# The last network of a decoder: six layers as one stream of 192 groups instead of sections per layer

## The chip, the cores and the metric

One core of a Trainium2 chip runs the whole program. The metric is the device time of one execution in microseconds (us). Three executions of the kernel before took 3035.06, 3035.88 and 3041.49 us; their median is 3035.88 us.

## The reference, cut to what matters

The program is a decoder of twelve blocks over `x` of 4 batches x 256 tokens x 128 channels. Only the last block, `L3_ffn`, is changed. It repeats six layers, each with its own weights; all arithmetic is float32:

```
for i in range(6):
    x = attn_layer(shift_tokens(x), ...) + x      # 16 heads of 64, windows of 32 tokens
    x = ffn_layer(shift_tokens(x), ...) + x       # layernorm, W1 (128 x 682), a * gelu(gate), W2 (341 x 128)

attn_layer:
    q, k, v = split(x @ Wqkv[i])                  # 128 -> 3 x 1024
    q, k = l2norm(q) * qs, l2norm(k) * ks         # per head of 64
    q = q * cos * scale + rotate_half(q) * sin * scale      # k with 1 / scale
    k = k * cos * inv   + rotate_half(k) * sin * inv
    out = softmax(q @ k.T * 8, masked to the own and the former window) @ v
    return out @ Wo[i]                            # 1024 -> 128
```

`shift_tokens` takes the upper half of the channels from the token before. The batches don't touch each other anywhere in this block.

## The kernel before, in words

`l3_ffn` holds the six layers. Each is a sequence of sections (`nc.Block`), and between two sections all engines meet at a barrier. An engine runs its own instructions in order and waits on semaphores that the others raise.

1. **Shift** (lines 1844 to 1868): eight transposes of `xin` on TensorE, ScalarE and VectorE copy the halves of the channels into `xnT`.
2. **`attend`** (line 1940), one section with two parts. The first makes the projections in 16 steps (two halves of 512 columns x 8 tiles of 128 tokens). A step is a q, a k and a v matmul of 512 columns (lines 2094, 2099), two squares on ScalarE (2203), and on VectorE the sum of squares per head (2249), its guard, the reciprocal of its root (ScalarE's Sqrt is line 2208) and two multiplies that put the normed q and k into `unit` (2264). The second part walks 32 groups; a group is one pair of heads of one batch, and the loop runs over the pairs outside and the batches inside. A group is, on TensorE, four transposes of q and k as they are (2165), four transposes of `sin_rows` (2177), the mask and 8 score matmuls (2111, 2116), four transposes of the probabilities (2132) and 6 value matmuls (2148). GpSimd makes `sin_rows`, the halves swapped times the sine table (2075), and multiplies the probabilities by `inverse` (2082). VectorE takes the negated maximum (2271), multiplies by the cosine table (2275), adds the two turned parts (2282), copies the turned probabilities (124) and inverts the sums (2294). ScalarE does four Exp with their sums (2222) and stores the heads (122). Behind the last group come the out projections of the four batches, 16 matmuls each (2190), added to `xin` (2298). All the weights of the output and the GLU arrive during this section.
3. **Late shift and norm**: three matmuls with a shift matrix (1895 to 1897), then `norm` with its statistics on VectorE, a Sqrt on ScalarE and transposes (325), with 20 matmuls that keep TensorE busy (229).
4. **GLU**: `chunk_block` with six gate matmuls, Gelu on ScalarE (1916), six value matmuls, multiplies on VectorE (1919), and 24 down matmuls (1928).

The next `w_qkv` is loaded in section 3. PSUM has eight banks; in `attend` the projections use six for q and k and two for v, and the groups use three for turning, two for scores, two for the turned probabilities and one for the heads.

## Time and profile before

| | |
|---|---|
| median of three executions | 3035.88 us |
| the profiled execution, its own time | 3039.18 us |
| its span, first to last instruction | 3037.4 us |
| TensorE busy over the span | 2697.1 us (89%) |
| VectorE | 1861.4 us (61%) |
| ScalarE | 1445.9 us (48%) |
| GpSimd | 994.7 us (33%) |
| mean granted clock of TensorE | 0.938 |

The profile shows one execution. "PE" is TensorE's matmuls, "PEld" its weight loads, which run beside the matmuls, "DVE" VectorE, "ACT" ScalarE and "POOL" GpSimd. A float32 matmul stands as two instructions (two weight loads and two matmuls), a transpose as one. The duration of one instruction holds a fill and a drain that overlap with its neighbours, so what an instruction costs its engine when work is queued is the distance from its start to the next start. The bracket at the end of a row is idle time of the engine before it and what ended it. The clock is the share of full speed (2.4 GHz) that TensorE was granted.

### The profile page before, as it was taken

The page shows a single profiled execution, that of the slowest core. Times are in us where ns is not written, and L with a number is a line of the kernel's source. Part 1 is how long each engine was busy: PE and PEld are TensorE (multiplying, and loading weights), DVE is VectorE, ACT ScalarE, POOL GpSimd, SP SyncE. Part 2 cuts the span into 40 slices and gives each one's busy share as a digit, 9 for nine tenths or more (in the row PEclk, how much of TensorE's full clock was granted, in tenths as well). Part 3 has the DMA queues.
Part 4 walks back from the last instruction along what each step waited for, and adds up shares of the span by engine and source line. Part 5 has one row for each costly group of instructions (what it writes and reads, how often), then busy time and mean ns, then how long its engine had stood idle before and what let it go on. Part 6 is the DMA issues. An engine that isn't in the chain of part 4 may idle for free. (4 is left out here: it accounts for less than half of the span.)

```text
span 3037.4 us, 59204 instructions
## 1 busy us (share of the span) xinstructions
PE 2697.1 (89%) x20645; PEld 1729.4 (57%) x20645; DVE 1861.4 (61%) x4106; ACT 1445.9 (48%) x4868; POOL 994.7 (33%) x1103
## 2 busy tenths in 40 slices
PE   5999969799989889783899978999999999999898
PEld 3555546455556556462455544856847647567476
DVE  3566665455567545556355558858677588586774
ACT  1455537326567456331255545545454355354553
POOL 0344435104456333100044431604406226044061
PEclk8799989898989999895799999999999999999999
DMA  2000000000000000000000001010010010100100
GB/s 66 1 0 0 0 8 2 20 26 1 5 1 2 4 28 0 6 1 7 26 1 0 0 32 46 2 46 19 12 53 2 22 42 2 49 15 23 42 2 29
DMA packets 41958, 48.85 MB, mean 16 GB/s; under 512 B 11963, under 2 KB 31301, under 8 KB 40838
## 3 DMA queue, kind: packets, MB, share of 16 engines
q1 hardware_dynamic: 41734, 45.89, 5.3%
q8 instruction: 138, 2.26, 0.3%
q14 instruction: 86, 0.70, 0.1%
HBM read 32.76 MB, written 0.52 MB: 11 GB/s over the span
## 5 line engine op out<-in xcount | busy, mean ns | idle before, releaser
L2075 POOL TENSOR_TENSOR net_sin_rows<-net_unit_qk,net_sin_table 128x512 f32<-128x512 f32 x192 | 243.8, 1270 | 649.8 <-PE bank L2177 375.3
L2222 ACT ACTIVATE net_probs<-bank,net_negmax 128x96 f32<-128x96 f32 x768 | 251.0, 339 | 302.4 <-DVE net_negmax L2271 302.4
L1022 POOL TENSOR_TENSOR l_probs<-l_probs,rowinv 128x512 f32<-128x512 f32 (+2 forms) x256 | 192.4, 772 | 571.8 <-DVE rowinv L1034 571.0
L1042 DVE TENSOR_REDUCE negmax<-scores 128x1 f32<-128x508 f32 (+4 forms) x512 | 212.8, 467 | 220.0 <-PE scores L919 180.2
L1022 POOL TENSOR_TENSOR lora_probs<-lora_probs,rowinv 128x508 f32<-128x508 f32 (+1 forms) x256 | 149.5, 617 | 253.3 <-DVE rowinv L1034 253.3
L987 ACT ACTIVATE l_probs<-scores,negmax 128x512 f32<-128x512 f32 (+2 forms) x256 | 139.5, 550 | 169.8 <-DVE negmax L1042 169.0
L124 DVE COPY turned<-flip 128x512 f32<-128x512 f32 (+3 forms) x280 | 163.0, 582 | 75.5 <-PE flip L946 65.9
L2094 PE MATMUL bank<-net_w_qkv,xnT 128*128 128x512 f32 x384 | 196.8, 637 | 7.5 <-PEq L1845 7.2
L734 DVE TENSOR_REDUCE negmax<-scores 128x2 f32<-128x256 f32 (+2 forms) x192 | 157.8, 822 | 66.3 <-PE scores L642 36.7
L919 PE MATMUL scores<-kT,qM 64*128 64x512 f32 (+2 forms) x768 | 190.2, 572 | 6.3 <-ACT kT L122 2.3
L987 ACT ACTIVATE lora_probs<-scores,negmax 128x508 f32<-128x508 f32 (+1 forms) x256 | 117.8, 472 | 132.2 <-DVE negmax L1042 131.4
L2082 POOL TENSOR_TENSOR net_probs<-net_probs,net_inverse 128x384 f32<-128x384 f32 x192 | 158.8, 827 | 51.6 <-DVE net_inverse L2294 51.6
L122 ACT ACTIVATE turned<-flip 128x512 f32<-128x512 f32 (+3 forms) x280 | 143.3, 512 | 59.2 <-PE flip L656 49.1
L2271 DVE TENSOR_REDUCE net_negmax<-bank 128x4 f32<-128x384 f32 x192 | 106.6, 555 | 104.2 <-PE bank L2116 104.2
L969 PE MATMUL heads<-turned,V 128*64 128x256 f32 (+1 forms) x1280 | 166.3, 381 | 2.0 <-ACT turned L122 1.3
L2116 PE MATMUL bank<-net_qk_T 64*64 64x96 f32 (+1 forms) x3072 | 162.5, 246 | 0.0
L2222 ACT ACTIVATION_READ_ACCUMULATOR net_probs<-bank,net_negmax 128x1 f32 x768 | 156.1, 203 | 0.0
L2116 PEld LDWEIGHTS bank<-net_qk_T 64*64 64x64 f32 x3072 | 125.7, 135 | 51.1 <-issue 51.1
L2177 PE MATMUL bank<-ident,net_sin_rows 128*128 128x128 f32 x768 | 121.5, 283 | 35.5 <-DVE net_cos_T L2275 35.3
L2203 ACT ACTIVATE net_probs_turned<-bank 128x512 f32<-128x512 f32 x192 | 114.0, 597 | 80.4 <-PE bank L2094 80.4
L124 DVE COPY net_probs_turned<-bank 128x512 f32<-128x512 f32 x192 | 130.6, 680 | 27.2 <-PE bank L2132 27.2
L2282 DVE TENSOR_TENSOR net_qk_T<-bank,net_cos_T 128x512 f32<-128x512 f32 x192 | 132.8, 692 | 18.0 <-issue 0.4
(399 smaller groups left out, 6144.0 us busy)
## 6 DMA issues: line engine op xcount, KB each, us to landing
net_w_qkv<-in_L_ffn_Wqkv SPq DMA_DIRECT2D x7, 1536.0 KB, 6.6
net_vals_between<-net_vals SPq DMA_DIRECT2D x48, 192.0 KB, 2.5
net_w_out<-in_L_ffn_Wo SPq DMA_DIRECT2D x6, 512.0 KB
net_vals_between<-net_vals SPq DMA_DIRECT2D x48, 64.0 KB, 1.9
moe_w<-in_L_ffn_w13T SPq DMA_DIRECT2D x8, 256.0 KB, 2.7
net_w<-in_L_ffn_W SPq DMA_DIRECT2D x6, 341.0 KB
moe_w<-in_L_ffn_w2T SPq DMA_DIRECT2D x8, 128.0 KB, 2.2
ctx_tok<-in_ctx SPq DMA_DIRECT2D x1, 768.0 KB, 6.5
```

The lines of the kernel that those rows point to most:

```text
L124: return nc.vector.tensor_copy(dst, src)
L734: nc.vector.tensor_reduce(negmax[:, c:c + 2], scores[:, 2 * half:2 * half + 2, 0:nk], AX.X, ALU.max, negate=True).then_inc(maxed.sem, 1)
L919: last = nc.tensor.matmul(scores[:, 2 * qt + h, 0:nk], qM[rows, 0, t * P:(t + 1) * P], kT[rows, k0:k0 + nk], start=True, stop=cross)
L969: last = nc.tensor.matmul(heads[rows, q0 * P:QT * P], V[:, v0 + j, rows], turned[:, 2 * p + h, c0:c0 + w], start=(j == 0), stop=(j == part ...
L987: last = nc.scalar.activation(pr[:, slot(g, qt, h), k0:k1], scores[:, 2 * qt + h, k0:k1], ACT.Exp, bias=negmax[:, u * tail + w:u * tail + ...
L1022: last = nc.gpsimd.tensor_tensor(own, own, rowinv[:, u * tail + w:u * tail + w + 1].to_broadcast([P, k1 - k0]), ALU.mult)
L1042: last = nc.vector.tensor_reduce(negmax[:, u * tail + w:u * tail + w + 1], scores[:, 2 * qt + h, k0:k1], AX.X, ALU.max, negate=True)
L2075: nc.gpsimd.tensor_tensor(halves(sin_rows[:, g % 2, :, :, :]), halves(tiles_of_group(g))[:, :, ::-1, :], sin_table[:, :, :, :, :].rearrang ...
L2082: nc.gpsimd.tensor_tensor(prob_blocks(g), prob_blocks(g), part, ALU.mult).then_inc(shared.sem, 1)
L2094: nc.tensor.matmul(qk_bank(u, s), own, w_qkv[:, s * INNER + c * BANK:s * INNER + (c + 1) * BANK], start=True, stop=True).then_inc(filled.s ...
L2116: last = nc.tensor.matmul(bank[rows_of(h), SCORE_BANKS[g % 2], first:(w + 1) * KEYS], qk_T[rows_of(h), g % 3, 0, w * QB:(w + 1) * QB], qk_ ...
L2222: last = nc.scalar.activation(prob_blocks(g)[:, w, :], score_blocks(g)[:, w, :], ACT.Exp, bias=maxima[:, g % 4, w:w + 1], accum_out=sums[: ...
```

## The change

The six layers become one section, `stream`, of ticks. Tick s does, for group s, the scores, the maximum and the Exp, and besides it fixed shares of the work of other groups, each engine in a written order. A job is one batch of one layer; there are 24 jobs of 8 groups each, 192 groups in all, and the ticks run from -10 to 203. In every two ticks stands one step of 128 tokens x 512 columns of a later job's projections (q in the even tick, k and v in the odd one), and once in eight ticks the shift, the out projection, the late shift, the norm and the three parts of the GLU of one job, at ticks `SHIFT`, `OUT`, `LATE`, `ZT`, `GATES`, `BOTH`, `UPS` and `DOWN` of the job.

- The rotation is made on the rows, ahead of the turn and ahead of the division by the norm: VectorE multiplies the projection by the cosine table and, with halves swapped, by the sine table (`part`), GpSimd adds the two (`add_parts`) and multiplies each group by the inverse norms. One set of four transposes turns the sum, and one copy moves it from PSUM, on ScalarE for even and on VectorE for odd groups. The sine rows, their transposes, the multiply and the add behind the turn are gone.
- The inverse roots of the head norms (32 values per partition, once in four ticks) and of the layer norm (2 values per partition, once in eight) are made on GpSimd in 14 instructions each, every one waiting for the one before it (`inverse_root`). ScalarE's Sqrt and VectorE's reciprocals of norms are gone.
- The v matmul, the shift, the out projection, the late shift, the norm's turn and the GLU's matmuls share one PSUM bank, `spare`. `take_spare` makes TensorE wait until the user before has read it.
- q and k have one bank each, the turn has one, the turned probabilities have one.
- Gelu is one instruction of 768 columns per job, in the same queue as the Exp of every tick. The gates are first moved to SBUF with their bias.
- The tables per layer are made by GpSimd in three instructions. The matmuls that keep TensorE busy are gone. `w_qkv` is loaded in two halves of columns per layer.

The core of the diff (the removed lines are `attend` and the sections, printed above):

```diff
+def inverse_root(pool, src, floor, out, temp, step, before):
+    half, y, t = temp[:, 0, :], temp[:, 1, :], temp[:, 2, :]
+    done = [before]
+    def then(ins, last=False):
+        done[0] += 1
+        ins.then_inc(step.sem, 1)
+        if not last:
+            pool.wait_ge(step.sem, step.at(0, done[0]))
+    then(nc.gpsimd.tensor_scalar(half, src, floor, -0.5, ALU.max, ALU.mult))
+    then(nc.gpsimd.tensor_scalar(y.bitcast(I32), half.bitcast(I32), -0.5, ROOT_MAGIC, ALU.mult, ALU.add))
+    for r in range(3):
+        then(nc.gpsimd.tensor_tensor(t, y, y, ALU.mult))
+        then(nc.gpsimd.tensor_tensor(t, t, half, ALU.mult))
+        then(nc.gpsimd.tensor_scalar(t, t, 1.5, None, ALU.add))
+        then(nc.gpsimd.tensor_tensor(y if r < 2 else out, t, y, ALU.mult), last=(r == 2))
...
+    JOBS, PER = DEPTH * B, PAIRS
+    G, S = JOBS * PER, JOBS * 4
+    SHIFT, PROJ = -10, -8
+    SCALE, TURN, FLIP, VALUES = 2, 1, 2, 3
+    OUT, LATE, ZT, GATES, BOTH, UPS, DOWN = 12, 13, 15, 16, 17, 18, 19
+    TICKS = range(SHIFT, PER * (JOBS - 1) + DOWN + 1)
...
+        qk_bank = (bank[:, 0, :], bank[:, 1, :])
+        turn_bank, flip_bank = bank[:, 3, :], bank[:, 6, :]
+        heads = bank[:, 7, 0:N]
+        spare = bank[:, 2, :]
...
+            held = []
+            def take_spare():
+                for sig, count in held:
+                    pe.wait_ge(sig.sem, sig.at(0, count))
+            for s in TICKS:
+                u = at_tick(s, PROJ, 2, S)
+                if u is not None:
+                    m, c, t = step_of(u)
+                    l, b = job(m)
+                    if u % 4 == 0:
+                        pe.wait_ge(shift_lower.sem, shift_lower.at(0, m + 1))
+                        pe.wait_ge(shift_upper.sem, shift_upper.at(0, m + 1))
+                    if b == 0 and t == 0:
+                        pe.wait_ge(qkv_in[c].sem, qkv_in[c].at(l, 1))
+                    until(pe, parted, 2 * u - 1)
+                    nc.tensor.matmul(qk_bank[0], xnT[:, (QT * b + t) * P:(QT * b + t + 1) * P], w_qkv[:, half_cols(c)],
+                                     start=True, stop=True).then_inc(q_filled.sem, 1)
+                u = at_tick(s, PROJ + 1, 2, S)
+                if u is not None:
+                    m, c, t = step_of(u)
+                    l, b = job(m)
+                    own = xnT[:, (QT * b + t) * P:(QT * b + t + 1) * P]
+                    until(pe, parted, 2 * u)
+                    nc.tensor.matmul(qk_bank[1], own, w_qkv[:, INNER + c * BANK:INNER + (c + 1) * BANK],
+                                     start=True, stop=True).then_inc(k_filled.sem, 1)
+                    take_spare()
+                    nc.tensor.matmul(spare, own, w_qkv[:, 2 * INNER + c * BANK:2 * INNER + (c + 1) * BANK],
+                                     start=True, stop=True).then_inc(v_filled.sem, 1)
+                    held = [(v_copied, u + 1)]
                 g = s
                 if 0 <= g < G:
+                    until_copied(pe, g)
+                    until(pe, exped, g - 1)
...
+                g = s + TURN
+                if 0 <= g < G:
+                    m, c = group(g)
+                    pe.wait_ge(scaled.sem, scaled.at(0, g + 1))
+                    until_copied(pe, g - 1)
+                    for k in range(2):
+                        for q in range(QT):
+                            last = nc.tensor.transpose(turn_bank[:, (k * QT + q) * P:(k * QT + q + 1) * P],
+                                                       rope[:, m % 3, q, k, cols_of(c)], ident[:, :])
+                    last.then_inc(turned.sem, 1)
...
+                n = at_tick(s, BOTH, PER, JOBS)
+                if n is not None:
+                    take_spare()
+                    k = GT[2]
+                    nc.tensor.matmul(spare[0:k, 0:N], w1[:, GLU + 2 * P:GLU + 2 * P + k], znT[:, :], start=True, stop=True)
+                    nc.tensor.matmul(spare[0:k, N:2 * N], w1[:, 2 * P:2 * P + k], znT[:, :], start=True, stop=True).then_inc(both_made.sem, 1)
+                    held = [(gated_up, 3 * n + 1)]
...
+            def square(u, s, filled):
+                act.wait_ge(filled.sem, filled.at(0, u + 1))
+                until(act, reduced, u - 1)
+                nc.scalar.activation(squares[:, u % 2, s, :], qk_bank[s], ACT.Square).then_inc(squared.sem, 1)
...
+                n = at_tick(s, GATES, PER, JOBS)
+                if n is not None:
+                    act.wait_ge(gates_made.sem, gates_made.at(0, n + 1))
+                    until(act, gated_up, 3 * n)
+                    for j in range(2):
+                        affine("act", gelu[:, j, :], spare[:, j * N:(j + 1) * N], 1.0, vec[:, 5 + j:6 + j]).then_inc(gates_moved.sem, 1)
+                n = at_tick(s, BOTH, PER, JOBS)
+                if n is not None:
+                    k = GT[2]
+                    act.wait_ge(both_made.sem, both_made.at(0, n + 1))
+                    affine("act", gelu[0:k, 2, :], spare[0:k, 0:N], 1.0, vec[0:k, 7:8]).then_inc(gates_moved.sem, 1)
+                    act.wait_ge(gates_moved.sem, gates_moved.at(0, 3 * n + 3))
+                    nc.scalar.activation(gelu[:, :, :], gelu[:, :, :], ACT.Gelu).then_inc(gelued.sem, 1)
...
+            def add_parts(u, s):
+                m, c, t = step_of(u)
+                own = rope[:, m % 3, t, s, half_cols(c)]
+                pool.wait_ge(parted.sem, parted.at(0, 2 * u + s + 1))
+                nc.gpsimd.tensor_tensor(own, own, sin_parts[:, (2 * u + s) % 4, :], ALU.add).then_inc(added.sem, 1)
...
+            for s in TICKS:
+                g = s - 1
+                if 0 <= g < G:
+                    pool.wait_ge(inverted.sem, inverted.at(0, g + 1))
+                    part = inverse[:, g % 4, :].rearrange("p (w o) -> p w o", o=1).to_broadcast([P, BLOCKS, KEYS])
+                    nc.gpsimd.tensor_tensor(prob_blocks(g), prob_blocks(g), part, ALU.mult).then_inc(shared.sem, 1)
+                g = s + SCALE
+                if 0 <= g < G:
+                    m, c = group(g)
+                    j = g // 4
+                    pool.wait_ge(added.sem, added.at(0, 4 * j + 4))
+                    pool.wait_ge(rooted.sem, rooted.at(0, ROOT_OPS * (j + 1)))
+                    own = rope[:, m % 3, :, :, cols_of(c)].rearrange("p t s (h d) -> p (t s) h d", d=DH)
+                    factor = head_inv[:, j % 2, :].rearrange("p (ts h o) -> p ts h o", ts=4, o=1)[:, :, 2 * (c % 4):2 * (c % 4) + 2, :]
+                    nc.gpsimd.tensor_tensor(own, own, factor.to_broadcast([P, 4, 2, DH]), ALU.mult).then_inc(scaled.sem, 1)
+                j = at_tick(s, PROJ + 5, 4, S // 2)
+                if j is not None:
+                    pool.wait_ge(reduced.sem, reduced.at(0, 2 * j + 2))
+                    inverse_root(pool, head_sums[:, j % 2, :], 1e-24, head_inv[:, j % 2, :], head_temp, rooted, ROOT_OPS * j)
+                n = at_tick(s, LATE + 1, PER, JOBS)
+                if n is not None:
+                    pool.wait_ge(spread_in.sem, spread_in.at(0, n + 1))
+                    inverse_root(pool, ln_sum[:, :], LN_EPS, ln_inv[:, :], ln_temp, ln_rooted, ROOT_OPS * n)
+                u = at_tick(s, PROJ + 1, 2, S)
+                if u is not None:
+                    add_parts(u, 0)
+                u = at_tick(s, PROJ + 2, 2, S)
+                if u is not None:
+                    add_parts(u, 1)
...
+            def part(u, s):
+                m, c, t = step_of(u)
+                l, b = job(m)
+                if u % (4 * B) == 0 and s == 0:
+                    dve.wait_ge(tabled.sem, tabled.at(0, 3 * (l + 1)))
+                dve.wait_ge(squared.sem, squared.at(0, 2 * u + s + 1))
+                raw = qk_bank[s].rearrange("p (h d) -> p h d", d=DH)
+                nc.vector.tensor_tensor(rope[:, m % 3, t, s, half_cols(c)].rearrange("p (h d) -> p h d", d=DH), raw,
+                                        cos_table[:, l % 2, t, s:s + 1, :].to_broadcast([P, HB, DH]), ALU.mult)
+                until(dve, added, 2 * u + s - 3)
+                swapped = qk_bank[s].rearrange("p (h f d) -> p h f d", f=2, d=DH // 2)[:, :, ::-1, :]
+                table = sin_table[:, l % 2, t, s:s + 1, :].rearrange("p o (f d) -> p o f d", f=2).to_broadcast([P, HB, 2, DH // 2])
+                nc.vector.tensor_tensor(sin_parts[:, (2 * u + s) % 4, :].rearrange("p (h f d) -> p h f d", f=2, d=DH // 2), swapped, table,
+                                        ALU.mult).then_inc(parted.sem, 1)
...
+                g = s + TURN
+                if 0 <= g < G and g % 2 == 1:
+                    dve.wait_ge(turned.sem, turned.at(0, g + 1))
+                    until(dve, scored, g - 1)
+                    copy("dve", qk_T[:, g % 2, :, :].rearrange("p s n -> p (s n)"), turn_bank).then_inc(copied["dve"].sem, 1)
+                u = at_tick(s, PROJ + 2, 2, S)
+                if u is not None:
+                    j = u // 2
+                    dve.wait_ge(squared.sem, squared.at(0, 2 * u + 2))
+                    until(dve, rooted, ROOT_OPS * (j - 2) + 1)
+                    nc.vector.tensor_reduce(head_sums[:, j % 2, u % 2 * 2 * HB:(u % 2 + 1) * 2 * HB],
+                                            squares[:, u % 2, :, :].rearrange("p s (h d) -> p (s h) d", d=DH), AX.X,
+                                            ALU.add).then_inc(reduced.sem, 1)
...
```

## Rows read from the trace of the kernel before

**Rows 1.** Windows, one layer; per engine busy us (x instructions), PE clock, DMA share, GB/s

```profile
...
2222.00:2423.00 201.00, 188.20 (x1650) 128.78 (x1650) 141.94 (x290) 96.05 (x368) 66.98 (x65) 0.97 0.08 25
...
```

**Rows 2.** Windows of the same layer: projections, the 32 groups, the rest

```profile
...
2228.00:2276.00 48.00, 47.47 (x108) 18.95 (x108) 42.17 (x80) 31.17 (x64) 3.00 (x3) 0.97 0.22 61
2276.00:2393.00 117.00, 110.61 (x1376) 89.86 (x1377) 85.33 (x169) 55.52 (x291) 63.02 (x62) 0.97 0.02 4
2393.00:2429.00 36.00, 30.35 (x169) 20.20 (x167) 14.21 (x42) 9.37 (x13) 0.95 (x1) 1.00 0.12 44
...
```

**Rows 3.** Timeline, one group, TensorE's weight loads: start us, us, instruction

```profile
...
2333.29 0.64 PEld L2116 LDWEIGHTS bank<-net_qk_T 64*64 64x64 f32 x16 [0.26 <-issue]
...
2334.05 0.42 PEld L2132 LDWEIGHTS bank<-ident,net_probs 128*128 128x128 f32 x4
...
2334.63 0.20 PEld L2148 LDWEIGHTS bank<-net_probs_turned,net_vals 128*64 128x64 f32 x4 [0.17 <-issue]
...
2335.23 0.42 PEld L2165 LDWEIGHTS bank<-ident,net_unit_qk 128*128 128x128 f32 x4
...
2335.62 0.47 PEld L2177 LDWEIGHTS bank<-ident,net_sin_rows 128*128 128x128 f32 x4
...
2336.06 0.10 PEld L2111 LDWEIGHTS bank<-net_window,ident 128*128 128x128 bf16 x1
...
2336.42 0.64 PEld L2116 LDWEIGHTS bank<-net_qk_T 64*64 64x64 f32 x16 [0.26 <-issue]
...
```

**Rows 4.** Timeline, the same group, VectorE and ScalarE

```profile
...
2334.17 0.56 DVE L2271 TENSOR_REDUCE net_negmax<-bank 128x4 f32<-128x384 f32 x1 [0.51 <-PE bank L2116]
...
2334.64 0.68 DVE L2275 TENSOR_TENSOR net_cos_T<-bank,net_cos_table 128x512 f32<-128x512 f32 x1
2334.76 0.34 ACT L2222 ACTIVATE net_probs<-bank,net_negmax 128x96 f32<-128x96 f32 x1 [1.46 <-DVE net_negmax L2271]
...
2336.02 0.68 DVE L124 COPY net_probs_turned<-bank 128x512 f32<-128x512 f32 x1
2336.04 0.39 ACT L122 ACTIVATE net_unit_qk<-bank 128x256 f32<-128x256 f32 x1
...
2336.62 0.17 DVE L2294 RECIPROCAL net_inverse<-net_sums 128x4 f32<-128x4 f32 x1
...
```

**Rows 5.** Timeline, two matmuls of the projections, TensorE

```profile
...
2232.45 1.88 PE L2094 MATMUL bank<-net_w_qkv,xnT 128*128 128x512 f32 x4
...
2234.17 1.02 PE L2099 MATMUL bank<-net_w_qkv,xnT 128*128 128x512 f32 x2
...
```

**Rows 6.** Timeline, out projection of one batch, and the last matmuls of the GLU

```profile
...
2387.27 3.65 PEld L2190 LDWEIGHTS bank<-net_w_out,net_unit_qk 128*128 128x128 f32 x32
...
2420.59 5.43 PEld L1928 LDWEIGHTS bank<-net_w,net_unit_qk 128*128 128x128 f32 x48 [1.77 <-issue]
...
```

**Rows 7.** GpSimd by line and form: count | busy us, mean ns | idle before

```profile
...
L2075 POOL TENSOR_TENSOR net_sin_rows<-net_unit_qk,net_sin_table 128x512 f32<-128x512 f32 x192 | 243.8, 1270 | 649.8 <-PE bank L2177 375.3 <-DVE net_unit_qk L2264 274.4
L2082 POOL TENSOR_TENSOR net_probs<-net_probs,net_inverse 128x384 f32<-128x384 f32 x192 | 158.8, 827 | 51.6 <-DVE net_inverse L2294 51.6
...
L1022 POOL TENSOR_TENSOR l_probs<-l_probs,rowinv 128x512 f32<-128x512 f32 x128 | 130.3, 1039 | 421.8 <-DVE rowinv L1034 421.8
...
L1022 POOL TENSOR_TENSOR lora_probs<-lora_probs,rowinv 128x4 f32<-128x4 f32 x128 | 25.8, 201 | 0.0
...
```

**Rows 8.** Groups by line of the last stage, VectorE and ScalarE

```profile
...
L2249 DVE TENSOR_REDUCE net_qk_norms<-net_probs_turned 128x16 f32<-128x1024 f32 x96 | 117.1, 1220 | 30.9 <-ACT net_probs_turned L2203 21.7 <-DVE net_unit_qk L2264 0.5
...
L1916 ACT ACTIVATE net_unit_qk<-bank,net_layer_cols 128x512 f32<-128x512 f32 (+1 forms) x36 | 24.7, 686 | 20.0 <-PE bank L457 19.6
...
L1916 ACT ACT_TABLE_LOAD x6 | 7.7, 1283 | 7.4 <-PEq L252 7.4
...
```

**Rows 9.** Timeline, first matmuls of the stage

```profile
...
1827.39 3.75 PE L2094 MATMUL bank<-net_w_qkv,xnT 128*128 128x512 f32 x4 [1.05 <-PEq L1845]
...
```

**Rows 10.** The chain that ended last

```profile
...
3032.08 1.22 DVE x L1237
```

More of the change, by code:

```diff
@@ new lines, in _ @@
+                        n = at_tick(s, LATE, PER, JOBS)
+                        if n is not None:
+                            l, b = job(n)
+                            first, second = (xin[:, QT * b + q, half:D] for q in range(QT))
+                            pe.wait_ge(out_added.sem, out_added.at(0, n + 1))
+                            take_spare()
+                            nc.tensor.matmul(spare[:, 0:half], late[:, 0, :], first, start=True, stop=True)
+                            nc.tensor.matmul(spare[:, half:D], late[:, 0, :], second, start=True, stop=False)
+                            nc.tensor.matmul(spare[:, half:D], late[:, 1, :], first, start=False, stop=True).then_inc(late_made.sem, 1)
+                            held = [(late_moved, n + 1)]
@@ new lines, in _ @@
+                        n = at_tick(s, ZT, PER, JOBS)
+                        if n is not None:
+                            l, b = job(n)
+                            pe.wait_ge(normed.sem, normed.at(0, 2 * n + 2))
+                            take_spare()
+                            for q in range(QT):
+                                last = nc.tensor.transpose(spare[:, q * P:(q + 1) * P], z[:, QT * b + q, :], ident[:, :])
+                            last.then_inc(z_turned.sem, 1)
+                            held = [(z_moved, n + 1)]
@@ new lines, in _ @@
+                        n = at_tick(s, UPS, PER, JOBS)
+                        if n is not None:
+                            take_spare()
+                            for j in range(2):
+                                last = nc.tensor.matmul(spare[:, j * N:(j + 1) * N], w1[:, j * P:(j + 1) * P], znT[:, :], start=True, stop=True)
+                            last.then_inc(ups_made.sem, 1)
+                            held = [(gated_up, 3 * n + 3)]
+                        n = at_tick(s, DOWN, PER, JOBS)
@@ new lines, in _ @@
+                        if n is not None:
+                            pe.wait_ge(gated_up.sem, gated_up.at(0, 3 * n + 3))
+                            take_spare()
+                            for q in range(QT):
+                                for j in range(3):
+                                    k = GT[j] + (j == 2)
+                                    last = nc.tensor.matmul(spare[:, q * D:(q + 1) * D], acts[0:k, j, q * P:(q + 1) * P], w2[0:k, j, :],
+                                                            start=(j == 0), stop=(j == 2))
+                            last.then_inc(down_made.sem, 1)
+                            held = [(down_added, n + 1)]
@@ L2295, in _ @@
[L2295 to L2298 removed]
+                            until(dve, summed, g - 2)
+                            copy("dve", flat_p[:, g % 3, :], flip_bank).then_inc(moved.sem, 1)
+                        g = s + TURN
@@ L2300, in store @@
+                        if n is not None:
+                            l, b = job(n)
+                            own = xin[:, QT * b:QT * (b + 1), :]
+                            dve.wait_ge(down_made.sem, down_made.at(0, n + 1))
+                            nc.vector.tensor_tensor(own, own, spare[:, 0:N].rearrange("p (t d) -> p t d", t=QT), ALU.add).then_inc(down_added.sem, 1)
         def store():
```

680 lines of the change are left out of this document (300 added, 380 removed).

## The prediction, made before the changed kernel was run

> **What bounds the kernel now.** I read the windows of one layer first. Each of the six layers takes 201 us; TensorE is busy 188.2 of them, VectorE 141.9, ScalarE 96.1 and GpSimd 67.0 [rows 1]. Then the same layer in three pieces [rows 2]: 48 us of projections, 117 us of groups and 36 us for the rest, and in each of them TensorE is the busiest (47.5, 110.6, 30.4 us). The timeline of a group says why the middle piece takes what it takes: the mask of one group starts at 2336.06 and its scores at 2336.42, the scores before that started at 2333.29, so a group is 3.13 us, and TensorE's only gaps are the short "issue" ones of 0.26 and 0.17 us [rows 3]. So the stage is bound by TensorE's queue, and 32 x 3.13 = 100 us of the 117 are that; the other 17 us are the filling and emptying of the pipeline, with a clock of 0.97. Time can be won by taking work from TensorE and by taking away the seams. It can be lost where one of the other queues, which now have to fit under it, becomes longer than TensorE's.
>
> **What each engine has to do per job.** I count eight ticks (one job of one layer, 24 of them), all work included.
>
> TensorE, by distances between starts. Of a group stay scores 0.76, flip 0.58, values 0.60, the turn 0.39 and the mask 0.36 [rows 3], 2.69 us; the sine transposes, 0.44 us, are gone. Eight groups: 21.5. Projections: a step has three matmuls as before; four instructions from 2232.45 to 2234.17 are 1.72 us, so 0.86 per matmul [rows 5], 12 per job: 10.3. Out projection: 3.65, as it is [rows 6]. Down: 12 of the 48 instructions of 5.43 us [rows 6], 1.4. GLU's six matmuls of 256 columns, half of 0.86 each: 2.6. Late shift, shift and turn of z are ten instructions of about 0.11 us: 1.1. The sum is 40.5 us per job, against 201 / 4 = 50.25 now.
>
> VectorE: per tick a maximum at 0.47 (2334.17 to 2334.64), the copy of the turned probabilities at 0.60 (2336.02 to 2336.62), two 512-wide multiplies at 0.60 each, the reciprocal at 0.17 [rows 4]; every second tick the turn's copy, 0.60, and the sum of squares, 1.22 [rows 8]. That is 2.44 + 0.91 = 3.35 per tick, 26.8 per job, and with 5 us for the norm, the GLU's multiplies, the shifts and the two adds 32. ScalarE: four Exp and their reads 1.28 (2334.76 to 2336.04), a store 0.39 [rows 4], a square 0.6, half a v copy and half a turn copy 0.6 (512 columns from PSUM; the Gelu of that size takes 0.69 [rows 8]), so 2.9 per tick and 23 per job, and 2.4 for the affines, 0.9 for the Gelu and 2 x 1.28 for two table loads [rows 8]: 29. Neither passes TensorE.
>
> GpSimd: per tick the division of the probabilities 0.83, and two operations on 512 elements, 1.04 each [rows 7] if laid out like line 1022, 1.27 if like line 2075; I take the first, since nothing reverses halves there: 2.9 per tick, 23.3 per job. Then 14 x 3 = 42 small dependent operations per job. No row shows these with 32 or 2 elements or as TENSOR_SCALAR; the nearest is the multiply of 4 elements at 0.20, and 0.20 to 0.83 over 4 to 384 elements gives 0.25 at 32 [rows 7]. Each waits for the one before, which no row of GpSimd shows; I add 0.05. So 28 x 0.30 + 14 x 0.25 = 12 us, and 35 per job. The ends: below 0.20 it can't be by the row, 42 x 0.20 = 8.4; above, 1.04, the time of 512 elements, 44. I take the low side because the 4-element row is nearest in size.
>
> **What the path adds to TensorE's 40.5 us.** Three things.
>
> (a) TensorE changes its kind of work and waits at more places: two more per tick (q, and the piece of the job). The same four transposes cost 0.39 as turn and 0.58 before a wait with 0.17 of "issue" [rows 3]. So between 0 and 0.19 for each of 16; I take 0.1: +1.6.
>
> (b) The loop of one tick. From the end of scores to the next scores either ScalarE turns (0.12 to the maximum, 0.47 to the Exp, 1.28, then the copy 0.6, then mask and scores 1.12: 3.7) or VectorE (0.12, 0.47, two multiplies 1.2, the flip's copy 0.6, the turn's copy 0.69, 1.12: 4.2) [rows 3, 4]. TensorE's own ticks are, from scores to scores, 5.3, 4.4, 5.3, 5.0, 8.1, 4.2, 4.7 and 3.8 us for ticks 0 to 7 of a job, the 8.1 being the out projection. So the loops alone cost nothing; the cover is the other work of TensorE, and it is thin in ticks 1, 5 and 7.
>
> (c) Two detours. The Gelu: its ScalarE work starts 2.6 us after the scores of tick 1 and takes 0.4 + 1.28 + 0.9, so it ends at 5.2, while VectorE waits for it with the maximum of tick 2 queued behind; that maximum comes 1.1 us late, and the next scores come at 5.4 instead of 5.3. The Exp's table load falls in ScalarE's slack. The norm: in tick 5 GpSimd makes a head root and in tick 6 the layer norm's root behind it; VectorE's tick 7 waits for it with its maximum queued behind. With 0.25 to 0.35 per operation the root lands 4.0 to 7.1 us after the scores of tick 6, VectorE could go on at 4.7, and after the two normed tiles (0.5) the scores of tick 8 come 4.1 to 6.5 after those of tick 7 instead of 3.8. I take +1.5 for both detours together.
>
> So a job is 40.5 + 1.6 + 1.5 = 43.6 us.
>
> On these table loads the Trainium skill's page "ScalarE: Activation LUTs", section "Table sets: the hidden batching unit", tells against the change: group activations by the set they need. Before, a layer has four loads (Sqrt twice, Exp, Gelu); after, each job has two, eight per layer. By my sum the 4 more per layer lie in ScalarE's free time. By the rule taken as cost, it is the rival below.
>
> **The sum.** 24 jobs at 43.6: 1046 us. The first 12 ticks have no out projection and GLU (8.7 us less of TensorE), the last 8 no projections (at most 8, since the loops take over): together 14 us less, 1032. Before the first scores: weights start and shift as now, and the first projection can start about where it does now, 1827 [rows 9]; eight ticks of projections with nothing beside them are bound by VectorE, 3.6 us per step, plus a root of 4 and a turn: scores at about 1843. After the last scores (1843 + 1032 - 4 = 2871): the group's own way out 5.3, out projection and add 4, and the chain of the former job's GLU and its own late shift, norm, root and GLU 22: 31 us, 2902, and a barrier: `add_all` at 2904. It now starts at 3032.08 [rows 10]. That is 128 us less: 3039.2 - 128 = 2911 for the profiled execution, and that one stands 3.3 us above the median, so about 2908; I say 2905.
>
> DMA: the same bytes. The next layer's weights have three to four ticks, 15 to 20 us, between their wait and their use, and the two halves of `w_qkv` come separately; now the whole of it comes within the third piece of a layer, 36 us at 44 GB/s [rows 2], with idle DMA beside it. I cost this at nothing; if it were late, six seams of some us each would show.
>
> **Rivals.**
> 1. Forecast as above, 0.68.
> 2. The detours add up (0.15). The one spare bank, the Gelu with its loads and the norm's root are serial across four engines, and a delay in one feeds the next tick. If both loads of each job land on the path, 24 x 2.57 = 62 us: 2967; with another 1 us per job of waits for the spare bank 2990. For it: ScalarE's queue holds the v copy and the moves behind the Exp, and TensorE's v matmul of the next tick waits for them. Against it: 2 us of slack in most ticks. The rule of the skill named above comes out here.
> 3. Slower than before (0.08). GpSimd's small operations. GpSimd's job is 23.3 + 42 c; it reaches TensorE's 43.6 at c = 0.48 us, and 48.9, where the gain of 128 us is gone, at c = 0.61. At c = 0.8 a job is 57 and the program takes 3225. Its place is the queue of GpSimd in ticks 1, 5 and 6, its sign TensorE waiting for `scaled` and `shared`. For it: no row shows a dependent chain on GpSimd, nor a TENSOR_SCALAR, nor the integer view. Against it: 0.20 for a short multiply. The skill's page "GPSIMD Engine Reference", section "2.1 Instruction dispatch", says that such an instruction passes software on every core and ends when all have answered; it gives no time for one this short, so it moves nothing here.
> 4. The cover is complete (0.09): TensorE never waits, 40.5 to 41.5 per job, and 2840 to 2855.
>
> That the change doesn't do what it says could only be so if one stream kept the seams, by a shift that waits for the same batch's GLU; three ticks lie between the two.
>
> **Numbers.** The range reaches from 41.5 us per job with its ramp (2855, less 10) to a job of 47 us (2985): 2845 to 2985. What is left out is the slow rival and the worst of the second, and a little below. 0.2%, 6 us, is about what a measurement of this kernel can tell from no change. Faster 0.90, within 0.02, slower 0.08.
>
> **What the profile after would show.** One tick in the middle of the stage should average 5.45 us with TensorE over 90% busy in it; 192 groups of POOL root operations near 0.25 to 0.3 us apart; the score groups of one job unevenly spaced, with about 8 us over the out projection; VectorE waiting for Gelu once per job for about 1 us and for the root of the norm once per job; 48 or 49 table loads at 1.28 us. The clock at 1.0 throughout, since no gap of 4 us is left in front of the groups. Wrong would be: GpSimd busy over 85% with TensorE waiting for it (rival 3), or TensorE waiting over 4 us per job for ScalarE and VectorE at the spare bank (rival 2).

## The result and the profile after

The changed kernel takes 3019.34 us (median of five, 3014.18 to 3021.76), against 3035.88 before in the same runs: a ratio of 0.9929, with a 95% interval of 0.9908 to 0.995. Faster, but by 17 us where 128 were forecast, and outside the range. The head of the page, in the order span, then busy time and share per engine:

```profile
span 3013.1 us, 59098 instructions
...
PE 2597.0 (86%) x20009; PEld 1658.7 (55%) x20009; DVE 1779.4 (59%) x3856; ACT 1535.5 (51%) x4987; POOL 1430.8 (47%) x2316
```

TensorE has 100 us less work than before, GpSimd 436 us more. Two jobs of the middle, in windows from the mask matmul of tick 0 to that of the next job's tick 0 (columns as in [rows 1]):

```profile
...
2451.89:2499.34 47.45, 41.97 (x387) 28.75 (x387) 32.02 (x62) 27.75 (x98) 34.53 (x67) 1.00 0.09 24
2402.93:2451.89 48.96, 43.48 (x387) 29.41 (x387) 32.02 (x62) 27.75 (x98) 36.03 (x70) 0.97 0.08 23
```

A job takes 47.45 us where 43.6 were forecast and 50.25 were spent before [rows 1]; five of the 24 take 49 us, at a mean clock of 0.97. The busy times of a job are those that were added up beforehand: VectorE 32.0 (forecast 32), ScalarE 27.8 (29), TensorE 42.0, in which overlaps are counted, for 40.5 between starts, and GpSimd 34.5. The 35 forecast for GpSimd held the gaps between its dependent operations; with these, 42 of 0.08 us, it is occupied for 38. So no engine had much more work than was counted. The time is in waits. These are the starts of the mask matmul (line 2073), one per tick, as distances in us; "walk" is the list in part (b) of the prediction with the late starts of (c):

```
tick of the job      0->1  1->2  2->3  3->4  4->5  5->6  6->7  7->0   job
walk                 5.3   4.4   5.4   5.0   8.1   4.2   4.7   4.1-6.5
changed kernel       5.33  4.46  8.08  4.94  8.03  4.22  6.75  5.63   47.45
  a job with a fall  5.33  4.47  8.98  5.55  8.03  4.22  6.75  5.63   48.96
```

Five ticks are right to a tenth. Tick 2 is 2.7 us too long and tick 6 2.0; tick 7 lies within its range. The list of waits for 1900 to 2900 us (who <- for whom, total us, times, longest) names what is late:

```profile
...
DVE net_acts L2425 <- ACT net_gelu L2269: 57.5, 21, 2.8
PE bank L2065 <- DVE net_acts L2431: 42.9, 21, 2.0
DVE z L2368 <- POOL net_ln_inv L1867: 39.7, 21, 1.9
PE bank L2065 <- DVE xnT L124: 38.4, 21, 1.8
...
PE bank L2140 <- DVE z L2368: 21.4, 21, 1.0
```

Line 2065 is the v matmul of an odd tick, which takes the spare bank. Around tick 2, TensorE:

```profile
...
2416.68 1.12 PE L2062 MATMUL bank<-net_w_qkv,xnT 128*128 128x512 f32 x2
2419.84 2.07 PE L2065 MATMUL bank<-net_w_qkv,xnT 128*128 128x512 f32 x2 [2.04 <-DVE net_acts L2431]
...
2422.16 1.24 PE L2078 MATMUL bank<-net_qk_T 64*64 64x64 f32 x16
```

and the other two engines at the same time:

```profile
...
2412.24 1.28 ACT L2269 ACT_TABLE_LOAD   x1
...
2414.48 0.48 DVE L2425 SCALAR_TENSOR_TENSOR net_acts<-bank,net_layer_cols,net_gelu 85x256 f32<-85x256 f32 x1 [2.73 <-ACT net_gelu L2269]
...
2414.96 0.53 DVE L2373 TENSOR_REDUCE net_negmax<-bank 128x4 f32<-128x384 f32 x1
...
2417.20 0.68 DVE L124 COPY net_qk_T<-bank 128x512 f32<-128x512 f32 x1
...
2417.80 1.21 DVE L2398 TENSOR_REDUCE net_head_sums<-net_squares 128x16 f32<-128x1024 f32 x1
...
2418.92 0.86 DVE L2431 SCALAR_TENSOR_TENSOR net_acts<-bank,net_layer_cols,net_gelu 128x256 f32<-128x256 f32 x2
```

VectorE waits 2.73 us for the Gelu (its load is the first row), and then does the maximum of tick 2, the rotation, two copies and the sum of squares. Only behind all these, at 2418.92, come the two multiplies that read the spare bank. The v matmul, behind which the scores of tick 3 stand, needs that bank and starts at 2419.84. TensorE has then been idle for 2.04 us, and in this job its clock is down: 2.07 us for two instructions. The job after it has the same wait and keeps its clock, 1.12 us:

```profile
...
2468.80 1.12 PE L2065 MATMUL bank<-net_w_qkv,xnT 128*128 128x512 f32 x2 [2.04 <-DVE net_acts L2431]
```

Around tick 6 to 7:

```profile
...
2394.36 0.24 POOL L1861 TENSOR_SCALAR net_ln_temp<-net_ln_sum 128x2 f32<-128x2 f32 x1
...
2395.79 0.43 DVE L124 COPY xnT<-bank 64x255 f32<-64x255 f32 x1
...
2396.36 1.10 PE L2065 MATMUL bank<-net_w_qkv,xnT 128*128 128x512 f32 x2 [1.83 <-DVE xnT L124]
...
2398.08 0.20 POOL L1867 TENSOR_TENSOR net_ln_inv<-net_ln_temp 128x2 f32<-128x2 f32 x1
...
2398.23 1.27 POOL L2289 TENSOR_TENSOR net_rope<-net_rope,net_sin_parts 128x512 f32<-128x512 f32 x1
...
2398.31 2.05 DVE L2368 TENSOR_SCALAR z<-z,meanvar,net_ln_inv 128x128 f32<-128x128 f32 x2 [1.89 <-POOL net_ln_inv L1867]
...
2400.39 0.56 DVE L2373 TENSOR_REDUCE net_negmax<-bank 128x4 f32<-128x384 f32 x1
...
2400.42 0.44 PE L2140 MATMUL bank<-ident,z 128*128 128x128 f32 x2 [1.02 <-DVE z L2368]
```

The same again: the shift's copy is last in VectorE's tick, and v waits 1.83 us. Then the norm: its statistics are ready at 2391.15, but GpSimd still has a sum, a division and a product in its queue, so the root runs from 2394.36 to 2398.28, 14 operations 0.28 us apart. It ends 6.7 us after the scores of tick 6. The two multiplies of `z` then take 2.05 us. Before, eight of these took 0.27 each on end. They start 0.08 us after a sum on GpSimd begins, and the maximum stands behind them.

GpSimd's groups in 1900 to 2900 us (busy, mean ns, idle before):

```profile
...
L2289 POOL TENSOR_TENSOR net_rope<-net_rope,net_sin_parts 128x512 f32<-128x512 f32 x169 | 214.5, 1269 | 0.0
L2307 POOL TENSOR_TENSOR net_rope<-net_rope,net_head_inv 128x512 f32<-128x512 f32 x169 | 177.0, 1047 | 0.0
L2297 POOL TENSOR_TENSOR net_probs<-net_probs,net_inverse 128x384 f32<-128x384 f32 x168 | 138.7, 826 | 194.9 <-DVE net_inverse L2349 194.9
L1866 POOL TENSOR_SCALAR net_head_temp<-net_head_temp 128x32 f32<-128x32 f32 x126 | 37.0, 294 | 11.0
...
L1865 POOL TENSOR_TENSOR net_ln_temp<-net_ln_temp 128x2 f32<-128x2 f32 x63 | 12.3, 195 | 5.0
...
L1862 POOL TENSOR_SCALAR net_head_temp<-net_head_temp 128x32 int32<-128x32 int32 x42 | 9.1, 216 | 3.5
```

Last, the end of the stage:

```profile
...
2987.89 0.23 POOL L1861 TENSOR_SCALAR net_ln_temp<-net_ln_sum 128x2 f32<-128x2 f32 x1 [20.64 <-DVE net_ln_sum L2361]
...
2991.59 0.19 POOL L1867 TENSOR_TENSOR net_ln_inv<-net_ln_temp 128x2 f32<-128x2 f32 x1
...
2991.82 0.60 DVE L2368 TENSOR_SCALAR z<-z,meanvar,net_ln_inv 128x128 f32<-128x128 f32 x2 [4.01 <-POOL net_ln_inv L1867]
...
2992.48 0.69 PE L2140 MATMUL bank<-ident,z 128*128 128x128 f32 x2 [5.94 <-DVE z L2368]
...
3004.05 2.90 PE L2177 MATMUL bank<-net_w,net_acts 128*128 128x128 f32 x12 [1.06 <-DVE net_acts L2431]
...
3007.73 1.23 DVE L1237 TENSOR_TENSOR x<-x,xin 128x1024 f32<-128x1024 f32 x1 [0.32 <-PEq L1973]
```

From the last mask matmul, 2961.5, to the final add it is 46 us. Nothing runs beside the last job's GLU, so TensorE works at half clock (2.90 us for 12 down instructions that take 1.50 in a middle job at full clock), and all of the root's 3.9 us are waited for. Here, with GpSimd idle, the two multiplies of `z` take 0.60 us.

### The profile page after: what moved, and what is told of

Read it like the earlier page. It is cut to its first block and busy times, and to the rows that moved or that the text cites. A ratio compares the mean times of both kernels' runs of the same rounds, so it can differ in the third digit from the quotient of the medians.

```text
span 3013.1 us, 59098 instructions
## 1 busy us (share of the span) xinstructions
PE 2597.0 (86%) x20009; PEld 1658.7 (55%) x20009; DVE 1779.4 (59%) x3856; ACT 1535.5 (51%) x4987; POOL 1430.8 (47%) x2316
## 5 line engine op out<-in xcount | busy, mean ns | idle before, releaser
L2289 POOL TENSOR_TENSOR net_rope<-net_rope,net_sin_parts 128x512 f32<-128x512 f32 x192 | 243.7, 1269 | 10.8 <-DVE net_sin_parts L2342 10.8
L2307 POOL TENSOR_TENSOR net_rope<-net_rope,net_head_inv 128x512 f32<-128x512 f32 x192 | 201.1, 1047 | 0.0
L2065 PE MATMUL bank<-net_w_qkv,xnT 128*128 128x512 f32 x192 | 107.5, 643 | 85.0 <-DVE net_acts L2431 42.9
L2206 ACT ACTIVATE net_squares<-bank 128x512 f32<-128x512 f32 x192 | 115.7, 603 | 71.6 <-PE bank L2062 39.8
L719 POOL TENSOR_TENSOR cross_probs<-cross_probs,rowinv 128x1024 f32<-128x1024 f32 x64 | 119.9, 1894 | 66.2 <-DVE rowinv L729 66.2
L2336 DVE TENSOR_TENSOR net_rope<-bank,net_cos_table 128x512 f32<-128x512 f32 x192 | 130.7, 681 | 8.8 <-ACT net_squares L2206 8.8
```

The costliest lines, as they stand in the source:

```text
L2289: nc.gpsimd.tensor_tensor(own, own, sin_parts[:, (2 * u + s) % 4, :], ALU.add).then_inc(added.sem, 1)
L2307: nc.gpsimd.tensor_tensor(own, own, factor.to_broadcast([P, 4, 2, DH]), ALU.mult).then_inc(scaled.sem, 1)
```

## The experiments

Each kernel was timed beside the kernel before on one chip, in three rounds, not all in one session. Times are medians; a ratio is against before in the same session. Between kernels of two sessions both are given where they differ. All edits are in `stream`. The distances of a typical middle job:

```
                        2->3   3->4   6->7   7->0    job          time     ratio
changed kernel          8.08   4.94   6.75   5.63    47.45, 49    3019.3   0.9929
x1_shift                8.1    6.55   4.72   8.68    51.2         3082.0   1.0143
x2_ups                  6.00   4.95   6.75   5.67    45.4         2968.1   0.9758
x3_max                  8.1-9  4.9-6  6.75   5.08    46.9, 48.5   3012.8   0.9914
x9_port                 8.1-9  5.7-6.5 6.75  4.22    47.6         2999.7   0.9869
x12_both                8.1-9  4.9-6.5 4.72  6.09    45.9, 47.5   3002.1   0.9885
x7_gelu                 7.01   4.94   6.75   5.64    46.4         2984.2   0.9835
x8_turns                7.65   5.38   6.75   5.20    48.8         3041.9   0.9998
x4_all                  5.78   4.95   4.72   7.4-8.5 44.9, 47.3   2986.5   0.9826
x5_order                5.77   4.95   4.72   5.63    43.3         2926.4   0.9618
x6_short                5.77   4.95   4.72   4.50    42.2         2891.6   0.9504
x10_heads               5.77   4.95   4.72   4.20    41.9         2881.2   0.9492
x11_turns               5.76   5.38   5.12   4.25    44.4         2945.9   0.971
```

**x2_ups: the GLU's multiplies earlier in VectorE's tick.** In `block.vector`, the block of `UPS` goes from behind `BOTH` to in front of the flip's copy:

```diff
+                        n = at_tick(s, UPS, PER, JOBS)
...
                         g = s - FLIP
```

> The changed kernel, with the two multiplies of the GLU that read the spare bank (tick 2) moved from the end of VectorE's tick to right behind the rotation multiplies. Theory A: the distance from tick 2 to tick 3 falls from 8.1 us to about 6.2, since the maximum of tick 2 still comes 1.1 us late behind the Gelu and the turn's copy now stands behind the multiplies; 22 jobs by 1.9 us are 42 us less, and some of the five jobs in which the clock falls keep it; about 2975. Theory B (the Gelu with its two table loads sets this tick): less than 10 us.

Tick 2 is 6.00, and 51 us are won: theory A. The falls of the clock (8 us) are gone with it, which is why it is more than 42.

**x1_shift: the shift's copy likewise,** the block of `SHIFT` in front of `g = s - FLIP`.

> The changed kernel, with VectorE's copy of the shifted halves (spare bank to xnT) moved from the end of tick 6 to right behind the two rotation multiplies. Theory A (the v matmul of an odd tick waits for a reader of the spare bank that VectorE has put behind all else of its tick): the distance of the mask matmuls from tick 6 to tick 7 falls from 6.74 us to about 4.7, what TensorE's own work takes; 23 jobs by 2.0 us are 47 us less, about 2972. Theory B (these ticks are long because GpSimd's chain of 14 operations and its sums are behind, and the spare bank only shows it): the wait moves to another semaphore and less than 10 us are won.

Tick 6 did fall to 4.72, and yet the kernel is 63 us slower. What was won in tick 6 came back in tick 7, 8.68, and with interest: ticks 6 and 7 together went from 12.38 to 13.40, tick 0 behind them from 5.33 to 6.45 and tick 3 to 6.55. One job of it in a window:

```profile
...
2479.00:2530.30 51.30, 46.05 (x387) 31.90 (x386) 32.02 (x62) 28.02 (x97) 34.58 (x67) 0.90 0.08 22
```

The clock is at 0.90: TensorE now gets to the end of tick 7 sooner, stands idle there until the root and the multiplies of `z` are through, and does what follows at half clock. Theory B was nearer here: behind the wait for the spare bank stood a chain of the same length, GpSimd's root and the multiplies of `z`.

**x3_max: the maximum of tick 7 ahead of the multiplies of `z`.**

```diff
+                        g = s
+                        if 0 <= g < G: ... nc.vector.tensor_reduce(maxima[:, g % 4, :], ...)
                         n = at_tick(s, ZT, PER, JOBS)
```

> The changed kernel, with the maximum of tick 7 ahead of the two multiplies that normalise z, not behind them. Theory A (the maximum stands in the queue behind a wait for the layer norm's root and behind two multiplies that take 1.03 us each where they took 0.27 before): the distance from tick 7 to tick 0 falls from 5.64 us to about 4.0; 23 by 1.6 are 37 us less, about 2982. Theory B (the turn of z and the affine behind it hold the next tick anyway): the distance stays over 5 us.

Tick 7 lies between the theories, 5.08, but the 7 us of the median are within the intervals of the two ratios, so no gain is shown. The turn of `z` stands in TensorE's queue and waits for the same multiplies, and the clock now falls in 12 jobs instead of 5.

**x9_port: GpSimd waits until VectorE is through with `z`.**

```diff
                             inverse_root(pool, ln_sum[:, :], LN_EPS, ln_inv[:, :], ln_temp, ln_rooted, ROOT_OPS * n)
+                            pool.wait_ge(normed.sem, normed.at(0, 2 * n + 2))
```

> The changed kernel with one wait more: in tick 6 GpSimd, behind the layer norm's root, waits until VectorE has normalised z before it adds the rotation's parts. Theory A (the two multiplies of z, which read and write SBUF, take 2.05 us instead of 0.53 because GpSimd's sum of 512 elements starts with them): they take about 0.55, the maximum behind them comes 1.5 us earlier, the distance from tick 7 to tick 0 falls from 5.64 to about 4.2, and GpSimd's sums stay at 1.27; about 33 us less, 2986. Theory B (the long duration is the wait for the root's second semaphore or z itself): the multiplies stay at 1 us each and the time is within 10 us of 3019.

Its timeline at that place:

```profile
...
2442.07 0.20 POOL L1867 TENSOR_TENSOR net_ln_inv<-net_ln_temp 128x2 f32<-128x2 f32 x1
...
2442.30 0.60 DVE L2369 TENSOR_SCALAR z<-z,meanvar,net_ln_inv 128x128 f32<-128x128 f32 x2 [1.92 <-POOL net_ln_inv L1867]
...
2442.98 1.28 POOL L2289 TENSOR_TENSOR net_rope<-net_rope,net_sin_parts 128x512 f32<-128x512 f32 x1 [0.72 <-DVE z L2369]
```

The multiplies take 0.60 together where they took 2.05, and GpSimd's sum is as long as before: theory A, and a wait added to a kernel makes it 20 us faster. The forecast was 33; the rest went to the clock, which now falls in 19 of the 21 full jobs (47.6 us; the two others take 46.04). The Trainium skill's page "SBUF — State Buffer", section "Who interferes with whom", says that VectorE and GpSimd share one pair of SBUF ports, that a tensor_scalar can run in a mode that takes both, and that the one that comes second is blocked for the whole instruction of the first. The trace agrees with it in kind: beside the sum, which had 1.19 us left to run, the multiplies took 1.45 us longer. No run shows the ports themselves.

**x12_both: x1_shift and x9_port in one.**

> The changed kernel with the shift's copy moved (x1_shift) and GpSimd's wait for z (x9_port). x1_shift alone lost 60 us: ticks 6 and 7 together went from 12.4 to 13.4 us. Theory A (tick 6 to tick 0 is one chain, VectorE's statistics, GpSimd's division and scaling, 14 dependent operations, the blocked multiplies, the maximum; the moved copy only let TensorE reach its end earlier and stand idle there, at half clock behind it): with the multiplies free the two ticks are 1.5 us shorter, 10.8 to 11.5, and the time is 2985 to 3010. Theory B (the copy itself is harmful where it stands): still above 3050.

10.81 us for ticks 6 and 7: theory A. The copy does no harm where it stands; the chain behind it did. But it does no good either: x9_port alone has 10.97 us in the two ticks and about the same time. Without the wait for the spare bank TensorE stands in front of the turn of `z` instead:

```profile
...
2449.46 0.44 PE L2140 MATMUL bank<-ident,z 128*128 128x128 f32 x2 [1.58 <-DVE z L2369]
```

**x7_gelu: a Copy in the Gelu's place, and so no table loads** (`ACT.Copy` for `ACT.Gelu`; this kernel leaves the Gelu out of the computation).

> The changed kernel with a Copy in place of the Gelu: the Gelu itself and both table loads of each job are left out, the rest stays. Theory A (the readers of the spare bank stand last in VectorE's tick; the Gelu only adds its delay in front): VectorE's maximum of tick 2 comes 1.1 us earlier, the distance from tick 2 to tick 3 falls from 8.1 to about 7.0 and is still over TensorE's own 5.3; 22 jobs by 1.1 plus the falls of the clock: 25 to 33 us less, about 2990. Theory B (the loads are the cause of that tick): about 5.4, 60 us or more less, under 2960.

Tick 2 is 7.01, and 35 us are won by the medians, 29 by the ratios, 8 of them by the clock: theory A. The Copy takes 0.84 us like the Gelu, so what is taken away is the loads alone: the two of a job, 2.57 us, cost 1.07 us of the path.

**x4_all: the three moves, and the Gelu's multiply behind the maximum of tick 2.**

> All three moves in one, and the multiply that waits for the Gelu moved from the end of tick 1 to behind the maximum of tick 2. Theory A: no reader of the spare bank and no maximum is late, TensorE sets the pace: distances 5.3, 4.5, 5.4, 4.9, 8.0, 4.2, 4.7 and 4.0 us, 41 us per job instead of 47.5, so 23 by 6.4 are 147 us less: about 2872. Theory B (GpSimd, 75% busy in the stage, or the loops over four engines give a floor of their own): not under 45 us per job, above 2960.

Neither. Ticks 1 and 3 to 6 are as walked and tick 2 takes 5.78, but tick 7 takes 7.4 in one job and 8.5 in the next, with a tick 0 of 6.5 behind the 8.5:

```profile
...
2392.33 2.05 DVE L2372 TENSOR_SCALAR z<-z,meanvar,net_ln_inv 128x128 f32<-128x128 f32 x2 [1.34 <-POOL net_ln_inv L1867]
...
2394.44 0.69 PE L2140 MATMUL bank<-ident,z 128*128 128x128 f32 x2 [3.03 <-DVE z L2372]
...
2396.11 1.88 PE L2053 MATMUL bank<-net_w_qkv,xnT 128*128 128x512 f32 x2
```

TensorE's turn of `z` waits 3.03 us for the multiplies, and the q matmul behind it is at half clock.

**x5_order: x4_all with GpSimd's wait of x9_port.**

> The kernel with all the moves of x4_all and the same wait. There the distance from tick 7 to tick 0 was 7.4 to 8.5 us, TensorE idle 3.03 us in front of the turn of z and at half clock behind it. Theory A (root of the norm, then multiplies blocked by GpSimd, then the turn in TensorE's queue): 1.5 us less idle and fewer falls of the clock, distance about 6.2; a job about 44 us, 2940 to 2950. Theory B (the root alone): no change against x4_all, 2987.

60 us less than x4_all, more than expected: tick 7 is 5.63 where 6.2 was forecast, and the clock stays up in most jobs. Theory A.

**x6_short: x5_order with two Newton steps for the layer norm's root** (`inverse_root(..., rounds=2)`, 10 operations).

> x5_order with two Newton steps for the layer norm's root, not three: four dependent operations on GpSimd less, 0.28 us each. If the root is still what TensorE's turn of z waits for, the distance from tick 7 to tick 0 falls by another 1.1 us, about 5.1, and 25 us are won against x5_order; if not, nothing.

Tick 7 is 1.13 us shorter, as expected (4.50; the 5.1 started from 6.2), and 35 us are won where 25 were forecast.

```profile
...
2396.71:2438.89 42.18, 41.41 (x387) 28.91 (x386) 30.76 (x62) 27.97 (x97) 33.67 (x63) 1.00 0.10 26
```

TensorE is busy 41.4 of 42.2 us at full clock.

**x10_heads: two steps for the heads' roots too.**

> x6_short with two Newton steps for the heads' roots too: eight dependent operations of 0.28 to 0.33 us less on GpSimd per job, 2.6 us. If GpSimd's length were still felt, up to 2.6 us per job; I expect that TensorE sets the pace (42.2 us per job, 41 of its own work) and the time stays within 6 us of 2892.

10 us less by the medians, a little more than the 6 expected. In a middle job it is 0.3 us, in tick 7, so TensorE does set the pace there; the first two jobs, which have fewer other things to do, are 4.8 us shorter together (32.5 and 37.5 us for 35.5 and 39.1). By the ratios it is 4 us, and the intervals overlap. Both kernels beat the changed one and the one before.

**x8_turns and x11_turns: the turn's four transposes twice,** in the changed kernel and in x6_short.

> The changed kernel with the four transposes of each group made twice into the same bank, 0.43 us of TensorE per tick more, as much as the change took away with the sine rows. Theory A (TensorE sets the pace in ticks 0, 1, 3, 4 and 5 and stands waiting in 2, 6 and 7): 5 x 0.43 per job, about 2.2, 23 jobs: 50 us more, 3069. If TensorE set it everywhere: 83 more. If the queues of the others did: under 15.

> x6_short with the four transposes of each group made twice, as x8_turns did to the changed kernel (22 us there). If TensorE now sets the pace in all ticks but those two where its idle time is left (2 and 0, 0.2 to 0.5 us each): 6 to 8 times 0.43 per job, 60 to 80 us more, 2950 to 2970.

The same extra 0.43 us per tick cost 22 us in the one and 54 in the other by the medians (21 and 63 by the ratios). x8_turns missed its 50: tick 2 and tick 7 got shorter by 0.43 each, so that the v and the mask start where they did, and the clock fell nowhere. A job of x11_turns:

```profile
...
2286.06:2330.49 44.43, 44.36 (x419) 32.40 (x418) 30.61 (x62) 28.31 (x98) 33.77 (x63) 1.00 0.12 34
```

With it TensorE is busy in 44.36 of 44.43 us. By the medians the expected 60 to 80 was a little high, by the ratios not: ticks 2 and 7 still took up theirs.

## Why the prediction was wrong, step by step

- **The work of each engine per job: right in the main.** GpSimd's small operation was the term with no row: 0.30 forecast for 32 elements, 0.34 measured (0.26 and a gap of 0.08), and 0.25 for 2 elements against 0.28. The sum of the rotation's parts took 1.27 us and not 1.04, the product 1.05. Together 38 us and not 35. (As written, ScalarE's loop in (b) adds up to 3.6 us, not 3.7, and TensorE's ticks to 40.8, not 40.5; neither matters.)
- **(a) Changes of work on TensorE: too dear.** +1.6 us per job were allowed; ticks 0, 1, 3, 4 and 5 show nothing of it.
- **(b) The loops: the first step that failed.** "So the loops alone cost nothing" counted TensorE, the maximum, the Exp and the turn's copy. It left out the loop through the spare bank: v of an odd tick waits for whoever read the bank last, in ticks 2 and 6 that is VectorE, and VectorE's reader was written last in its tick. In tick 2 this sets the time, 8.08 us for 5.4, and x2_ups wins 51 us by moving the reader. By the prediction's own numbers it could be had: 1.2 for the late maximum, 0.47 + 1.2 + 0.6 + 0.6 + 1.2 + 0.9 and then v, mask and scores gives 8.1. In tick 6 the wait is there too, 1.83 us, but by itself it costs nothing: without it the time comes back in tick 7 (x1_shift, x12_both).
- **(c) The Gelu: right in what it costs** (its ScalarE work started 2.4 us after the scores of tick 1, forecast 2.6, and the maximum was 1.1 late, though VectorE waited for it 2.7 us and not 1). **The norm: the second step that failed, by its size.** Ticks 6 and 7 take 12.38 us where TensorE's own work is 8.5; 1.4 of the +1.5 were for this. The root was near the late end, 6.7 us after the scores of tick 6 in a range of 4.0 to 7.1: not because an operation is slow, 0.28 us, but because it started 3.2 us after its input was there. With the spare bank and the multiplies out of the way (x12_both) the two ticks still take 10.81, 2.3 over. The other 1.5 were VectorE's multiplies beside GpSimd's sum, of which the prediction had no term (x9_port: 10.97). That tick 7 itself, 5.63, lies in the 4.1 to 6.5 is luck: 2.0 us of the chain had passed during the wait of tick 6.
- **The clock.** "At 1.0 throughout" failed. That no gap of 4 us is left did not keep the clock up. The kernel before had a gap of that length in front of its groups, with half clock behind it (four transposes in 1.09 us, 0.63 at full clock):

```profile
...
2280.24 1.09 PE L2177 MATMUL bank<-ident,net_sin_rows 128*128 128x128 f32 x4 [4.42 <-DVE net_cos_T L2275]
```

In the changed kernel waits of 2.04 us at v were followed by half clock in 5 of 21 full jobs. Why in these and not in the others stays open.
- **The sum.** The first mask matmul came at 1846.4, where the forecast had the scores at 1843: 3 more. A job lost 6.65 us to waits (2.8 in tick 2, 2.0 in tick 6, 1.8 in tick 7) where (a) and (c) had allowed 2.8 over TensorE's own 40.8: 3.85 more, 81 us for the 21 jobs from the third to the last but one. The clock took 8 (five jobs, 1.5 each), and the first two and the last job were 2 shorter than forecast. The end took 13 more (46 for 33); it runs at half clock and every step of it is on the path, but no run takes it apart. Together that is the 104 us from 2904 to 3007.7, to within 1. A tick averaged 5.93 us for the 5.45 forecast, and TensorE was 88% busy where over 90% was the sign.
- **The rivals.** Rival 2 is the nearest, and still too low with 2990. It named the bank, but put the wait on ScalarE's readers at 1 us per job; TensorE waited 3.87 us per job for VectorE's (42.9 + 38.4 us in 21 jobs), just under the 4 that was named as its sign. Its table loads are refuted as a cost of 2.57 us per job: x7_gelu shows 1.07. The rule that the prediction cites from the Trainium skill, to group activations by table set, concerns 46 loads of 1.28 us of ScalarE's time here; of the kernel's time it is worth these 1.07 us per job and the 8 of the clock. GpSimd as the bound (3) is refuted: 38 us per job with its gaps, and x10_heads gains next to nothing. Its queue still matters by where the root stands in it.

Of the change's parts, the sine transposes that it took away were 84 us of TensorE, but putting as many back into the changed kernel cost only 22. The rest of that gain was spent at the spare bank in tick 2 and in the chain of the norm. With the readers and the maximum moved, GpSimd held back and the root shortened (x6_short), the kernel takes 2892 us; what was forecast for the changed kernel was 2905.

## What to carry to other kernels

When a resource is handed round between engines, its time is set by where its reader stands in the reader's queue, so walk each such loop with everything written ahead of it, and not the busy times alone. Two waits of the same length can stand behind each other: taking the first away won nothing while the second stood (x12_both against x9_port), and with the second lengthened by a blocked engine it lost 63 us (x1_shift). No run shows what the move of the shift's copy is worth once the root is short. Short waits of the engine that sets the pace can cost twice, once as time and once as clock.

## What the runs showed of the hardware

- Two VectorE multiplies of 128 x 128 from SBUF to SBUF took 2.05 us where a GpSimd operation on SBUF started beside them, and 0.60 where it was held back; GpSimd's duration was 1.27 and 1.28. The two at the end of the changed kernel, with GpSimd idle, took 0.60 as well. The eight of the kernel before, with GpSimd idle, were 0.27 apart.
- A chain of dependent operations on 2 elements on GpSimd ran at 0.28 us each, of which 0.19 to 0.24 were the operation; on 32 elements at 0.34 on average, of which 0.22 to 0.33.
- Waits of 2.04 us without matmuls, once per job, were followed by half speed in 5 of 21 full jobs of the changed kernel and in 19 of 21 of x9_port, 1.5 to 1.6 us lost each time; in the full jobs of x6_short, where TensorE waits 0.5 us at most in front of the turn of `z`, in none.
- On GpSimd an add of 512 elements took 1.27 us with both inputs of full length, as did the multiply of the kernel before with one input's halves reversed [rows 7]. A multiply with a broadcast of 8 values took 1.05, and one with a single value 1.04 [rows 7]. So the time went with the form of the inputs, and neither with the reversed halves nor, as far as these rows go, with the operation.
